# A decoder layer on one core: the passage from attention groups to expert groups rebuilt

## What is computed

```
x = x + attention(layernorm(x))                 # channel attention, 256 x 256 probabilities per sequence
x = x + cross(layernorm(x), ctx)                # bidirectional attention flow against 375 context rows
x = x + experts(layernorm(x))                   # 8 routed experts + 1 shared expert

logits = h @ gate_w.T; scores = sigmoid(logits); scores_c = scores + correction_bias
groups of two experts ranked by their sum, best 2 of 4 groups kept, best 4 of 8 experts kept
cw = scores of the kept experts / their sum * 2.5          # per token and expert
out = sum_e cw[:, e] * (silu(h @ Wg[e]) * (h @ Wu[e])) @ Wd[e]  +  the same with the shared weights, weight 1
```

## Time and profile before

| | |
|---|---|
| time, median of 3 runs | 740.56 us (740.51 to 740.74) |
| the profiled execution | 736.82 us |
| its span, first to last instruction | 734.8 us |
| PE busy | 678.7 us (92%) |
| DVE, ACT, POOL busy | 67%, 47%, 33% |
| mean granted TensorE clock | 0.978 |
| group 7 of block 1 | from 359.2 us |
| end of block 1 | about 422 us |

### The profile page before, as it was taken

The page is one execution under the profiler, slowest core; times in us unless marked ns, Lnnn a source line. Parts: engine busy times, 40 slices in busy tenths (PEclk is TensorE's granted clock), DMA queues, the critical chain, the costliest instruction groups (busy, mean ns, idle before and its releaser), DMA issues. The chain is left out here.

```text
span 734.8 us, 11792 instructions
## 1 busy us (share of the span) xinstructions
PE 678.7 (92%) x3880; PEld 570.7 (78%) x3880; DVE 489.4 (67%) x1252; ACT 347.3 (47%) x793; POOL 244.5 (33%) x322
## 2 busy tenths in 40 slices
PE   3998989999999899999998758899999999999997
PEld 2767968788789687887886636788888888888886
DVE  5577785776776867767776864866566666676432
ACT  3745655567456565574555233433343433333331
POOL 2144254162442542525423302232322223232222
PEclk9999999999999999999999778999999999999999
DMA  7615043041150330512402084032323212030300
GB/s 215 156 28 165 2 114 105 25 138 54 50 167 0 110 107 25 144 48 56 137 0 76 1 255 172 8 129 67 116 87 115 86 72 106 23 143 30 117 29 29
DMA packets 50765, 64.43 MB, mean 88 GB/s; under 512 B 3800, under 2 KB 49416, under 8 KB 49840
## 3 DMA queue, kind: packets, MB, share of 16 engines
q1 hardware_dynamic: 50736, 64.06, 27.9%
HBM read 56.60 MB, written 7.45 MB: 87 GB/s over the span
## 5 line engine op out<-in xcount | busy, mean ns | idle before, releaser
L1375 POOL TENSOR_TENSOR sg<-sg,cw_wide 128x512 f32<-128x512 f32 x56 | 74.8, 1335 | 185.7 <-ACT sg L1332 177.1
L1336 ACT ACTIVATE a_hi<-af 128x512 fp32r<-128x512 f32 x63 | 39.8, 632 | 153.7 <-DVE af L1456 153.7
L75 PE MATMUL bank<-h_hi,w_lo 128*128 128x512 f32 x224 | 92.6, 413 | 6.8 <-DVE w_lo L1473 5.1
L76 PE MATMUL bank<-h_lo,w_hi 128*128 128x512 f32 x224 | 90.4, 404 | 0.0
L77 PE MATMUL bank<-h_hi,w_hi 128*128 128x512 f32 x224 | 90.0, 402 | 0.0
L1456 DVE TENSOR_TENSOR af<-bank,sg 128x512 f32<-128x512 f32 x63 | 43.3, 687 | 63.5 <-POOL sg L1375 60.3
L1461 DVE TENSOR_TENSOR a_lo<-af,a_hi 128x512 fp32r<-128x512 f32 x63 | 47.2, 749 | 34.9 <-ACT a_hi L1336 34.9
L75 PE MATMUL bank<-w_hi,a_lo 128*128 128x256 f32 x224 | 63.3, 283 | 0.4 <-ACT lgt L180 0.4
L76 PE MATMUL bank<-w_lo,a_hi 128*128 128x256 f32 x224 | 63.2, 282 | 0.0
L77 PE MATMUL bank<-w_hi,a_hi 128*128 128x256 f32 x224 | 63.1, 282 | 0.0
L805 POOL TENSOR_TENSOR wz_lo<-wz,wz_hi 128x512 fp32r<-128x512 f32 x32 | 42.3, 1333 | 46.7 <-ACT wz_hi L601 46.7
(11 more groups left out here) (220 smaller groups left out, 1874.9 us busy)
## 6 DMA issues: line engine op xcount, KB each, us to landing
cw_wide<-cw_scratch SPq DMA_DIRECT2D x7, 2048.0 KB, 7.1
ctxtf<-in_ctx_t SPq DMA_DIRECT2D x32, 375.0 KB
ctxf<-in_ctx SPq DMA_DIRECT2D x32, 375.0 KB
xt<-in_x SPq DMA_DIRECT2D x8, 448.0 KB, 9.6
x_scratch<-x2b SPq DMA_DIRECT2D x8, 448.0 KB, 3.2
x2n<-x_scratch SPq DMA_DIRECT2D x7, 512.0 KB, 4.6
x2t<-x_scratch SPq DMA_DIRECT2D x7, 512.0 KB, 3.9
out_dram<-x2t SPq DMA_DIRECT2D x7, 512.0 KB, 2.9
```

Of the source, the lines that this page charges most:

```text
L75: pe.matmul(dst, a_lo, b_hi, start=first, stop=False, **kw)
L76: pe.matmul(dst, a_hi, b_lo, start=False, stop=False, **kw)
L1336: act.activation(a_hi[n % (AHEAD + 1)][:, :], af[(p + n) % 2][:, :], ACT.Copy).then_inc(a_hi_ok, 1)
L1375: pool.tensor_tensor(sg[b][:, :], sg[b][:, :], cw_wide[p][:, ORDER[n], :], ALU.mult).then_inc(sgw_ok, 1)
```

## The change

Only the passage and one detail of block 2 change in what is done; groups 0 to 6 of block 1 keep their order of work.

- **LayerNorm of the first 512 tokens.** `x2n` is loaded directly behind the last context loads of group 6 (the wait asks for three counts of `x2_st`, which hold the stores of groups 0 and 1). `moments3` is the first thing on DVE in group 7, ahead of `score_max(0)`; `normalise3` comes after `score_max(1)`, `rstd3` on POOL after `wz_low(1)`. PE turns `h3` after `z_c(1)` of group 6, ahead of `probs_proj(0)`, once `v_copy(1)` is done (`v` and `h3` share the PSUM banks 6 and 7). ACT's `v_copy(1)` moves up to follow `probs_high(1)`.
- **Routing of the first tokens.** `logits` follow `attention_out(0)`, `turn_logits` follows `attention_out(2)`, `sum_logits` is in DVE's `c_rows` stretch, `route_groups` before `mneg`, `route_experts` after `x3_low(3)`.
- **Three experts ahead.** The shared weights and those of experts 0 and 1 are loaded ahead of `x2n`, into free parts of `wl_f` and a new buffer `w_f01`. Their splits: ACT's high parts before `exps(0)` (shared) and before `a_columns(3)` (0 and 1), POOL's low parts after `wz_low` and after `rstd2`. They are kept in the `wqkv` buffers.
- **gate_up early.** PE does the `gate_up` of the shared expert and of expert 0 after `z_x3(3)`, with `turn_cw` between them, and only then its own group's `z_c`. DVE takes over the low parts of `wz` (`wz_low_last`) from POOL.
- **Block 2.** The weights `cw` are stored in block 1. Block 2's SP begins with the spread of two experts' `cw`, then experts 2 and 3, the other six `cw` rows, experts 4 to 7. In every group the spread of `cw` is now two transfers (2 and 6 rows). In group 0 `split_low` follows `product`.
- To make room, buffers are shared: `wz` with `tmp`, `at` with `qg`, `nb_wide` with `ctw`, `qk_bias` with `x1`; `res` gets its own.

The core of the diff:

```diff
 # sync, ahead of the last group
-sp.wait_ge(c2q_mm, G * (NGRP - 1) + 1)
+sp.wait_ge(wl_lo_ok, 2)
 for half, w in enumerate((wg_s, wu_s)):
     sp.dma_start(gate_up_weights(shared_f)[:, half, :, :], ...).then_inc(shared_in, 16)
 sp.dma_start(shared_f[:, GU:GU + D], wd_s).then_inc(shared_in, 16)
-sp.wait_ge(x1_ok, G * NGRP)
-sp.wait_ge(x2_st, 16 * (NGRP - 1))
+for e in range(2):
+    for half, w in enumerate((wg, wu)):
+        sp.dma_start(gate_up_weights(w_f01[:, e, :])[:, half, :, :], ...).then_inc(w01_in, 16)
+    sp.dma_start(w_f01[:, e, GU:GU + D], wd[e]).then_inc(w01_in, 16)
+sp.wait_ge(x2_st, 16 * 3)
 load_norm(sp, 0)
 # tensor, last group
 z_c(i - 1, 1)
+if last_group:
+    pe.wait_ge(v_ok, KB * (i + 1))
+    turn_h3(pe, 0)
 probs_proj(0)
...
 z_x3(3)
 if last_group:
-    turn_h3(pe, 0)
+    pe.wait_ge(shared_lo_ok, 1)
+    pe.wait_ge(x3_ok, ev[G - 1])
+    gate_up_early(0, shared_hi[:, 0:GU + D], shared_lo[:, 0:GU + D])
+    turn_cw(pe, 0, h_bank[1])
+    pe.wait_ge(w01_lo_ok, 1)
+    gate_up_early(1, wqkv_hi[:, 0, :], wqkv_lo[:, 0, :])
     for j in range(G):
         z_c(i, j)
-    pe.wait_ge(gate_ok, 1)
-    logits(pe, 0, h3_hi0, h3_lo0)
 # scalar, last group
+if last:
+    act.wait_ge(shared_in, 48)
+    act.activation(shared_hi[:, 0:GU + D], shared_f[:, :], ACT.Copy).then_inc(shared_hi_ok, 1)
 exps(0)
...
 probs_high(1)
+if last:
+    v_copy(1)
 exps(3)
+if last:
+    h3_high(act, 0, h3_hi0)
 # vector, last group, after the early stretch shown below
 x3_low(3)
+if last:
+    route_experts(dve, 0)
...
+wz_sum(0)
+wz_sum(1)
+wz_low_last(0)
+wz_sum(2)
+wz_low_last(1)
+wz_sum(3)
+wz_low_last(2)
+wz_low_last(3)
 # block 2, sync
+sp.wait_ge(cw_st, 16)
+spread_early(0)
+load_expert(2)
+load_expert(3)
+spread_rest(0)
+for e in range(4, NEXP):
+    load_expert(e)
```

More of the change, by code:

```diff
@@ L176, in logits, with copy_logits, turn_logits @@
             last.then_inc(lg_mm, 1)
-        def copy_logits(act, g):
+        def copy_logits(act, g, b):
             act.wait_ge(lg_mm, g + 1)
-            act.activation(lgt[:, :], h_bank[0][0:2 * NEXP, :], ACT.Copy).then_inc(lgt_ok, 1)
+            act.activation(lgt[:, :], b[0:2 * NEXP, :], ACT.Copy).then_inc(lgt_ok, 1)
+        def turn_logits(pe, g):
+            for t in range(T):
+                last = pe.transpose(h_bank[1][:, t * 2 * NEXP:(t + 1) * 2 * NEXP], lgt[:, t * P:(t + 1) * P],
+                                    ident[0:2 * NEXP, 0:2 * NEXP])
+            last.then_inc(t_lg, 1)
@@ new lines, in turn_cw, with exp_logits, copy_cw @@
+        def turn_cw(pe, g, b):
+            pe.wait_ge(route, ROUTE_STEPS * (g + 1))
+            for t in range(T):
+                last = pe.transpose(b[0:NEXP, t * P:(t + 1) * P], cw[:, t, :], ident[:, :])
+            last.then_inc(t_cw, 1)
+        def exp_logits(act, g):
+            act.wait_ge(lg_ok, g + 1)
+            act.activation(den[:, :, :], lg[:, :, :], ACT.Exp, scale=-1.0).then_inc(eneg_ok, 1)
+        def copy_cw(act, g, b):
+            act.wait_ge(t_cw, g + 1)
+            if not is_first(g):
+                act.wait_ge(cw_st, 16 * g)
+            act.activation(cwt[:, :], b[0:NEXP, :], ACT.Copy).then_inc(cwt_ok, 1)
@@ L477, in c2q_product @@
                         for b in range(NSB):
-                            last = pe.matmul(bank[j][0:L, 0:D], at[:, j, b * L:(b + 1) * L], ctxf[0:SB, j, b, :], start=(b == 0),
+                            last = pe.matmul(bank[j][0:L, 0:D], at[j][:, b * L:(b + 1) * L], ctxf[0:SB, j, b, :], start=(b == 0),
                                              stop=(b == NSB - 1))
@@ L708, in group @@
                     probs_proj_copy(0)
-                    v_copy(1)
+                    if not last:
+                        v_copy(1)
                     probs_high(3)
@@ L727, in group @@
                     c_high()
+                    if last:
+                        for e in range(2):
+                            act.wait_ge(w01_in, 96)
+                            act.activation(wqkv_hi[:, e, :], w_f01[:, e, :], ACT.Copy).then_inc(w01_hi_ok, 1)
                     a_columns(3)
@@ L825, in group @@
                         ln1_scalars(i + 1)
+                    if last:
+                        for e in range(2):
+                            pool.wait_ge(w01_hi_ok, e + 1)
+                            pool.tensor_tensor(wqkv_lo[:, e, :], w_f01[:, e, :], f32(wqkv_hi[:, e, :]), ALU.subtract).then_inc(w01_lo_ok, 1)
                     pool.wait_ge(c_hi_ok, i + 1)
@@ L834, in group @@
                         pool.tensor_tensor(x2b[:, j, :], x1[:, j, :], bl_wide[:, :], ALU.add).then_inc(x1b_ok, 1)
-                    if last:
-                        rstd3(pool, 0)
-                        for j in range(G):
-                            wz_low(i, j)
                 pool.wait_ge(consts, 4)
@@ L975, in group @@
                         ln1_stats(i + 1, 2)
+                    if last:
+                        moments3(dve, 0)
                     score_max(0)
@@ L979, in group @@
                     score_max(1)
+                    if last:
+                        normalise3(dve, 0)
                     inv_sum(0)
@@ L991, in group @@
                     probs_low(2)
+                    if last:
+                        h3_low(dve, 0, h3_hi0, h3_lo0)
                     if is_first(i):
@@ L1015, in group @@
                     c_rows(1)
+                    if last:
+                        dve.wait_ge(wk_in, 48)
+                        sum_logits(dve, 0)
                     dve.wait_ge(st2_ok, ev[2])
@@ L1051, in group @@
                     dve.reciprocal(sinv2[:, :], ssum2[:, :]).then_inc(sinv2_ok, G)
+                    if last:
+                        route_groups(dve, 0)
                     dve.wait_ge(t_m, i + 1)
@@ L1085, in group @@
                     dve.wait_ge(q2c_ok, i + 1)
-                    for j in range(G):
-                        wz_sum(j)
-                    if last:
-                        normalise3(dve, 0)
-                        h3_low(dve, 0, h3_hi0, h3_lo0)
-                        dve.wait_ge(shared_hi_ok, 1)
-                        dve.tensor_tensor(shared_lo[:, 0:GU + D], shared_f[:, :], f32(shared_hi[:, 0:GU + D]), ALU.subtract).then_inc(shared_lo_ok, 1)
+                    if not last:
+                        for j in range(G):
+                            wz_sum(j)
+                    else:
+                        wz_sum(0)
[6 more added lines that the diff above has]
+                        wz_low_last(3)
                         x2_sum(i, 0)
@@ L1281, in group @@
                     for n in range(NE):
-                        gate_up(g, p, n)
-                        if n == 1 and is_first(g):
-                            turn_cw(0)
-                            pe.wait_ge(cwt_ok, 1)
+                        if not is_first(g) or n >= 2:
+                            gate_up(g, p, n)
                         if not last:
```

279 lines of the change are left out of this document (145 added, 134 removed).

## The result

The changed kernel takes 731.62 us (median of four runs, 728.13 to 742.18), the kernel before 740.53 beside it: ratio 0.987, 95% interval 0.9821 to 0.9918. Run again, unaltered, it took 729.65 us, ratio 0.9851 (0.9804 to 0.9897). The forecast was 727, range 718.5 to 733: right in sign and within its range. The gain was forecast at 13.7 us and came to 8.9, in the second set of runs to 10.5.

The account below looks back on a forecast made before the run. PE bounds the kernel, losing about 32 us to waits and low clock from group 7 to the second expert group. Running shifts of +11.0, 7 late at block 1's end, -5.9, -8.4 reach -13.7: 740.56 - 13.7, about 727, range 718.5 to 733.

Parts of the forecast that it names:

- What can be won: Group 7 to second expert group: PE's waits 20.8 us plus clock shortfall at most 11.7, about 32 us in all.
- B: Stretch from the start of block 1's last `x2_sum` to the second expert group's first `gate_up`; forecast 41.9 us.
- A: Stretch from group 7's first `scores` matmul to the start of block 1's last `x2_sum`; forecast 61.1 us.
- The last step of the sum: Block 2, -8.4 to -13.7 us: waits of 1.7 and 1.0 shrink to 0.3; half clock 1.65 and gaps 0.9 go.
- When `x2n` lands: Group 7: lands at about 371 (365 to 372.5), behind the context loads' tail, as `xt` did in group 5.
- rival 1: Group 7: `x2n` lands by 366, PE waits only 1.5 us at `turn_h3`; 719.5 us; chance 0.26.
- `normalise3` at 2.0 us: DVE in group 7: `normalise3` takes 2.0 us, from 2.32 beside POOL, less without it; ends at 376.7.
- The low clock after the wait: PE after its 7 us wait: `turn_h3` 1.6 and `probs_proj(0)` 2.6 us, 2 us more than at full clock.
- To `turn_x(0)`: From `turn_c(0)`: `sum_logits` adds 0.45 us, two ACT splits 1.0; `turn_x(0)` at 408.5, was 396.13.
- `route_groups`: nothing: DVE, group 7: its 11 steps, 2.8 us, fit into a 1.8 us wait and slack ahead of `mexp`, costing nothing.
- Rival 2: Smaller gain: `normalise3` and splits may take twice as long beside POOL, 3 to 8 us more; 733 us; chance 0.18.
- Rival 3: Slower: PE's clock stays low after the 7 us wait, +18 instead of +2; 743 to 745 us; chance 0.04.

Follow-up runs that it names:

- POOL held: One wait added on POOL behind `rstd3(0)` in the changed kernel, so its three subtractions start when `h3` is written: 725.38 us, ratio 0.980 to the kernel before.

## Why the prediction was right, and what it mis-sized

- *What can be won.* Right in kind: the waits for the low part, `mrow`, `h3_low` and `cw` went, the wait for `h3` in group 7 became one for `v`, that in block 2 stayed. B was forecast 41.9 us (103.05 - 61.14) and measured 41.9. That it fits to the digit is luck: B lies between 41.5 and 43.0 us in the eight profiles with the same order behind A. The wait for `h3` ahead of it, forecast 7, measured 6.9, is not luck; it is the same in every kernel that keeps that order. The last step of the sum is off: -8.4, 1.7 and 1.0 shrinking to 0.3, 1.65 and 0.9 add up to -13.4 and not -13.7; for the 1.65 and the 0.9 the prediction shows no row.
- *When `x2n` lands.* Forecast 371, 15.9 us after the last context issue at 355.07. Measured 372.61, 16.1 us after an issue at 356.52. The step that rested on the `xt` row held to 0.2 us, and rival 1 is out: even issued first, `x2n` came 13 us after the last context issue. The way there was another, so part of the fit is luck. From 360 to 365 us, first before, then changed:

```profile
360.00:365.00 5.00, 5.00 (x24) 3.92 (x23) 4.96 (x10) 2.51 (x5) 1.22 (x1) 1.00 0.33 112
```
```profile
360.00:365.00 5.00, 5.00 (x33) 4.25 (x32) 4.16 (x8) 1.14 (x2) 0.00 (x0) 1.00 0.64 193
```

  The weights did not wait for the tail but moved beside it, and then at 192 GB/s (365.0 to 372.6 us), not 283. SP issued `x2n` itself only at 367.60, since its ten issues lasted from 357.39 to 368.03, the first of them 3.56 us. The formula of the Trainium skill, DMA: Bandwidth & Descriptors, Anatomy of one DMA, put the landing 5.9 us after the first issue. That section gives it for transfers issued from GpSimd, these are issued by SP, and counted from the first issue in this trace, 357.39, it is 9.3 us too early.
- *`normalise3` at 2.0 us.* **The step that failed.** It took 4.75, and 1.38 with POOL held. I had 2.32 us from one row and wrote "less without it", without asking whether POOL would be beside it: the three subtractions stand directly behind `rstd3` on POOL, so they start in the very moment in which `normalise3` does. Against `scores` the wait ended 14.1 us later, forecast 13.0. It is 1.1 and not 2.75 because `x2n` came 2.9 us after the start of `scores` instead of my 4.1 (the spell of low clock at 355 us had delayed `scores` and not the transfers), and `normalise3` began 3.3 us behind it instead of 3.7.
- *The low clock after the wait*, counted at 2 us: `turn_h3(0)` to `turn_c(0)` took 13.9, forecast 13.1. 0.8 us short.
- *To `turn_x(0)`*: forecast 15.5, measured 14.7. 0.8 too much.
- *`route_groups`: nothing.* Wrong. With `gmask` and `choice` held by POOL it took 5.8 us instead of 2.8, and PE waited 1.0 us for `op_lo` at `z_c2q(0)` and 0.3 for `mrow`. `turn_x(0)` to the first `gate_up` took 10.8, forecast 9.4: 1.4 us.
- The errors add up: 1.1 + 0.8 - 0.8 + 1.4 = 2.5 of the 2.7 us missing in A. The two of 0.8 us cancel by luck. Rival 2 had named the mechanism, new work that takes twice as long beside POOL, at 3 to 8 us over the passage; it was there, at less than the near end.
- *What can be told apart.* The prediction put it at 0.2%, 1.5 us. The interval of its own ratio came out at 0.5% to either side, 3.6 us.
- *Rival 3*, a clock that stays low: the spell after the 7.9 us wait ended 5.6 us after PE resumed (383.81 to 389.4, by the pace of `probs_proj`). It did not decide.
- *Two `gate_up` ahead of the barrier*: I counted them as work done early. The trace agrees with the count but not with its use: without them the kernel is as fast.

Behind the failed step the Trainium skill has a rule, SBUF — State Buffer, Who interferes with whom: VectorE and GpSimd share one pair of ports under an exclusive lock, which a VectorE instruction needs in a two-port mode (`tensor_scalar` and copies) or with two inputs from SBUF against a GpSimd instruction that reads SBUF. "Whoever issues first gets the shared pair for the whole instruction". The held rows above agree (4.75, 1.77, 1.75, 2.19, 3.66 us) and so do those that were not held (0.37 us with an operand from PSUM). On who came first the rows are too rough to tell: `mrow` starts at 410.80, POOL's subtraction beside it at 410.85. As an estimate by that rule from the POOL rows of this trace, `normalise3` lasts as long as the POOL instructions beside it, 2.53 + 1.84 = 4.37 us, against the 4.75 measured.

## What to carry to other kernels

When work is moved to VectorE, write down what POOL runs in the same microseconds, and price each `tensor_scalar` and each instruction with two SBUF operands at the length of the POOL instruction beside it, not at its own; then hold POOL with one wait, but only if its work does not meet something dearer later. Work brought forward pays only if the chain behind the barrier is brought forward too: 5.6 us of matmuls gained nothing, and a wait of 6.9 us gave 0.9 us in the passage, 2.7 when one of the three waits behind it was moved too. Compare stretches from a landmark that the change cannot touch.
